# A product of values and output weights taken in 16-bit parts that POOL splits off, with a ring of two for masked blocks

## What is computed

```python
q = causal_conv_silu(x @ Wq); k = causal_conv_silu(x @ Wk)      # (b, t, 16, 128), then normalised
v = causal_conv_silu(x @ Wv)                                     # (b, t, 16, 256)
def step(state, inp):                                            # over the positions t
    qt, kt, vt, at, bt = inp
    state = state * at
    err = vt - einsum('bhkv,bhk->bhv', state, kt)
    state = state + bt * einsum('bhk,bhv->bhkv', kt, err)
    return state, einsum('bhkv,bhk->bhv', state, qt)
out = outs.reshape(b, t, 4096) @ Wo                              # 4096 = 16 heads x 256 values
x = x + out
```

## Time and profile before

| what | value |
|---|---|
| median of 3 runs | 1176.99 us |
| lowest, highest | 1175.23, 1182.03 us |
| profiled execution, its own time | 1187.94 us |
| span of its trace | 1186.1 us |
| mean granted TensorE clock | 0.945 |
| busy PE, DVE, ACT, POOL | 1057.7, 844.3, 721.0, 442.2 us |
| share of the span | 89%, 71%, 61%, 37% |

### The profile page before, as it was taken

One profiled execution on the slowest core, in us unless ns is written; L12 is line 12 of the kernel. 1 busy time (PEld: TensorE's weight loads), 2 busy tenths in 40 slices (PEclk: granted clock), 3 DMA queues, 4 the chain that ended last, 5 costly groups with the idle time before them and its releaser, 6 DMA issues.

```text
span 1186.1 us, 24906 instructions
## 1 busy us (share of the span) xinstructions
PE 1057.7 (89%) x8176; PEld 714.3 (60%) x8176; DVE 844.3 (71%) x1427; ACT 721.0 (61%) x1284; POOL 442.2 (37%) x574
## 2 busy tenths in 40 slices
PE   3589999999999999999899999998887889996987
PEld 3257777777777776777677677776554334443444
DVE  4768888877888877888688788877544656663354
ACT  3367777777776776767677676776332345555221
POOL 5254544535445453553435355436201122223000
PEclk9889999999999999999999999999997679998788
DMA  6002000010000000000000100000000040000001
GB/s 182 20 1 63 2 28 28 1 28 0 27 27 1 27 0 27 27 0 27 3 28 1 28 27 0 10 1 1 1 1 1 1 75 1 2 2 22 1 1 36
DMA packets 30359, 22.44 MB, mean 19 GB/s; under 512 B 3014, under 2 KB 29318, under 8 KB 30139
## 3 DMA queue, kind: packets, MB, share of 16 engines
q1 hardware_dynamic: 27547, 16.89, 4.9%
q0 software_dynamic: 2720, 4.42, 1.8%
HBM read 22.94 MB, written 1.05 MB: 20 GB/s over the span
## 4 chain that ended last, share of the span: by engine, by line
PE 61%; DVE 13%; ACT 12%; issue 10%; POOL 1%; DVEq 1%; DMA 1%; SPq 0%; ACTq 0%; POOLq 0%
PE psum L1121 10%; PE psum L1179 5%; DVE y L877 4%; PE psum L1147 4%; PE psum L1260 4%; PE psum L1298 3%; PE psum L1273 3%; PE psum L1199 3%; ACT L648 2%; PE psum L1137 2%; PE psum L1207 2%; PE psum L1457 2%; ACT kq L648 2%; ACT sq L651 2%; DVE ux L842 2%
## 5 line engine op out<-in xcount | busy, mean ns | idle before, releaser
L434 POOL TENSOR_TENSOR ct<-lm,levels 128x512 f16<-128x512 f32 x224 | 253.1, 1160 | 261.1 <-DVE lm L887 261.1
L877 DVE SCALAR_TENSOR_TENSOR y<-psum,cwh,y 128x508 f32<-128x508 f32 (+2 forms) x384 | 284.4, 741 | 17.6 <-ACT y L604 8.6
L842 DVE TENSOR_TENSOR ux<-ux,psum 128x512 f16<-128x512 f16 x192 | 130.7, 681 | 46.5 <-PE psum L1208 46.4
L1137 PE MATMUL psum<-wo,vt 128*128 128x256 f32 x512 | 127.4, 393 | 1.9 <-DVE y L877 1.4
L604 ACT ACTIVATE y<-psum,cwh 128x512 f32<-128x512 f32 x128 | 99.0, 774 | 37.7 <-PE psum L1121 37.7
L579 ACT ACTIVATE t1c<-psum 128x256 f16<-128x256 f32 x192 | 73.1, 380 | 63.0 <-PE psum L1199 61.9
L724 ACT ACTIVATE et<-psum 128x1024 f32<-128x1024 f32 x64 | 65.6, 1025 | 62.6 <-PE psum L1442 62.5
L1137 PEld LDWEIGHTS psum<-wo,vt 128*128 128x128 f32 x512 | 94.5, 195 | 12.8 <-DVE y L877 1.6
L991 DVE TENSOR_REDUCE mx<-psum 128x4 f32<-128x1024 f32 x64 | 77.7, 1221 | 28.8 <-PE psum L1421 28.6
L1199 PE MATMUL psum<-ux,ct 128*128 128x128 f16 x768 | 97.5, 221 | 0.6 <-ACT t1c L579 0.6
L856 DVE TENSOR_TENSOR ux<-ux,psum 128x512 f16<-128x512 f16 x128 | 87.6, 685 | 14.3 <-PE psum L1208 11.8
(11 more groups left out here) (209 smaller groups left out, 2346.0 us busy)
## 6 DMA issues: line engine op xcount, KB each, us to landing
wraw<-in_L_attn_Wv SPq DMA_DIRECT2D x32, 128.0 KB, 2.7
wo<-in_L_attn_Wo SPq DMA_DIRECT2D x16, 256.0 KB, 2.8
wraw<-in_L_attn_Wk SPq DMA_DIRECT2D x16, 128.0 KB, 2.5
wraw<-in_L_attn_Wq SPq DMA_DIRECT2D x16, 128.0 KB, 2.7
x<-in_x SPq DMA_DIRECT2D x8, 128.0 KB, 5.2
maskrow<-in_mask_row POOLq DMA_DIRECT2D x1, 1024.0 KB, 4.6
xt<-in_ctx SPq DMA_DIRECT2D x1, 1024.0 KB, 6.0
out<-x SPq DMA_DIRECT2D x8, 128.0 KB, 1.8
```

The source lines that it names most:

```text
L434: g.tensor_tensor(ct[:, st.c % 4, l], lm[:, st.c % 4, :, 0, :], levels[:, l, :].unsqueeze(1).to_broadcast([P, NB, T]), ALU.mult).then_inc( ...
L842: v.tensor_tensor(u, u, pr, ALU.subtract).then_inc(uxb_sb, 1)
L877: v.scalar_tensor_tensor(out=y[:, n, :, sh:], in0=u[:, :, 0:T - sh], scalar=cwh[:, (a.c // 2) % 2, n, TAPS - 1 - sh:TAPS - sh], in1=y[:, n ...
L1137: mm = t.matmul(ubank[n][:, j * H:(j + 1) * H], vt[:, r, vc, (2 * n + j) * T:(2 * n + j + 1) * T], wo[:, hr, vc, :], start=(vc == 0), stop ...
```

## The change

- A new POOL helper `split_wo` (three operations of 128 x 512) scales the weights `wo` by 64 and splits them into `woh` and `wol`, 16 bits each. It runs in odd slots, once for a head.
- A new POOL helper `split_v` (two operations of 128 x 1024) splits `vt` of step b0 into `vth` and `vtl`. It runs in every slot. Both stand behind `parts` and `split`, and ahead of the cuts of levels 4 to 6.
- `z(n)` makes three 16-bit products (`vth` x `woh`, `vth` x `wol`, `vtl` x `woh`) in place of each 32-bit one. It waits for `v_split` and `wo_split` in place of `silu` and the load. `zcopy` scales by 1/64.
- `vt` has one place in place of two: `v_silu` of a step waits for `split_v` of the step before. `ct` has two places in place of four: a cut waits for level 6 of two steps before.
- SP's load of `wo` waits for `wo_split` of the head two before, in place of z.

```diff
--- before.py
+++ after.py
@@ -181,9 +181,13 @@
         whi = lb("whi", [P, 2, TILES, CH, P], F16)
         wlo = lb("wlo", [P, 2, TILES, CH, P], F16)
         wo = lb("wo", [P, 2, 2, H], F32)
+        woh = lb("woh", [P, 2, 2, H], F16)
+        wol = lb("wol", [P, 2, 2, H], F16)
         y = lb("y", [P, TILES, NB, T], F32)
         kq = lb("kq", [P, 2, NB, 2, T], F32)
-        vt = lb("vt", [P, 2, 2, TOK], F32)
+        vt = lb("vt", [P, 2, TOK], F32)
+        vth = lb("vth", [P, 2, 2, TOK], F16)
+        vtl = lb("vtl", [P, 2, 2, TOK], F16)
         sq = lb("sq", [P, NB, 2, T], F32)
         n2m = lb("n2m", [P, 2, NB], F32)
         lnn = lb("lnn", [P, 2, NB], F32)
@@ -193,7 +197,7 @@
         rows = lb("rows", [P, P], BF16)
         decay = lb("decay", [P, NB, 2, T], F32)
         lm = lb("lm", [P, 4, NB, 2, T], F32)
-        ct = lb("ct", [P, 4, LEVELS, NB, T], F16)
+        ct = lb("ct", [P, 2, LEVELS, NB, T], F16)
         ux = lb("ux", [P, 2, NB, 2, T], F16)
         t1b = lb("t1b", [P, NB, T], F16)
         t1c = lb("t1c", [P, NB, T], F16)
@@ -280,6 +284,7 @@
         x0_full, res_psum, res_sb, y0_psum, y0_sb, y_psum, y_sb, out_psum, added = [sem(n) for n in (
             "x0_full", "res_psum", "res_sb", "y0_psum", "y0_sb", "y_psum", "y_sb", "out_psum", "added")]
         z_psum, z_sb = sem("z_psum"), sem("z_sb")
+        v_high, v_split, wo_high, wo_split = [sem(n) for n in ("v_high", "v_split", "wo_high", "wo_split")]
 
         xdone, result = sem("xdone"), sem("result")
         kv_names = ("ctx_loaded", "ctx_masked", "mask_cast", "mask_ready", "bias_cast", "bias_ready", "k_psum", "k_high", "k_stack", "v_psum", "v_ready")
@@ -362,7 +367,7 @@
                         need(sp, w_split, nxt.head)
                         load_w(nxt.head)
                         if nxt.c // 2 >= 2:
-                            sp.wait_ge(z_psum, nxt.at(-4).count(2, 4))
+                            sp.wait_ge(wo_split, nxt.head - 1)
                         load_wo(nxt.head, (nxt.c // 2) % 2)
 
             slots(sp, slot)
@@ -418,6 +423,30 @@
                 pool.wait_ge(w_high, h * 2 + 2)
                 g.tensor_tensor(wlo[:, ring].rearrange("p n c t -> p (n c t)"), w, wh, ALU.subtract).then_inc(w_split, 1)
 
+            def split_wo(st):
+
+                h, ring = st.head, (st.c // 2) % 2
+                pool.wait_ge(wo_loaded[ring], 16 * (st.c // 4 + 1) if st.i is None else st.i * 16 + 16 * (st.c // 4 + 1))
+                need(pool, z_psum, st.at(-4).count(2, 4))
+                w = wo[:, ring].rearrange("p v n -> p (v n)")
+                wh, wl = [q[:, ring].rearrange("p v n -> p (v n)") for q in (woh, wol)]
+                g.tensor_tensor(w, w, c64[:].to_broadcast([P, 2 * H]), ALU.mult).then_inc(wo_high, 1)
+                pool.wait_ge(wo_high, h * 2 + 1)
+                g.tensor_tensor(wh, w, zero[:].to_broadcast([P, 2 * H]), ALU.add).then_inc(wo_high, 1)
+                pool.wait_ge(wo_high, h * 2 + 2)
+                g.tensor_tensor(wl, w, wh, ALU.subtract).then_inc(wo_split, 1)
+
+            def split_v(st):
+
+                if not st.valid():
+                    return
+                pool.wait_ge(silu, st.count(2, 2))
+                need(pool, z_psum, st.at(-2).count(2, 2))
+                f, hi, lo = vt[:].rearrange("p v n -> p (v n)"), vth[:, st.c % 2].rearrange("p v n -> p (v n)"), vtl[:, st.c % 2].rearrange("p v n -> p (v n)")
+                g.tensor_tensor(hi, f, zero[:].to_broadcast([P, 2 * TOK]), ALU.add).then_inc(v_high, 1)
+                pool.wait_ge(v_high, st.count(1, 1))
+                g.tensor_tensor(lo, f, hi, ALU.subtract).then_inc(v_split, 1)
+
             pool.wait_ge(conv_scaled, 3)
             pool.wait_ge(xn_done, B)
             split(0, 0, None)
@@ -429,9 +458,9 @@
                     if not st.valid():
                         return
                     pool.wait_ge(lm_done, st.count(2, 2))
-                    need(pool, t1c_psum, st.at(-4).count(6, 6))
+                    need(pool, t1c_psum, st.at(-2).count(6, 6))
                     for l in levels_:
-                        g.tensor_tensor(ct[:, st.c % 4, l], lm[:, st.c % 4, :, 0, :],
+                        g.tensor_tensor(ct[:, st.c % 2, l], lm[:, st.c % 4, :, 0, :],
                                         levels[:, l, :].unsqueeze(1).to_broadcast([P, NB, T]), ALU.mult).then_inc(masked, 1)
 
                 cut(b, range(2, 4))
@@ -450,6 +479,9 @@
                     nxt = k.at(4)
                     first = k.i is None and k.c <= -2
                     split(nxt.head, (nxt.c // 2) % 2, None if first else nxt.at(-4))
+                if k.c % 2 == 1 and b0.valid():
+                    split_wo(b0)
+                split_v(b0)
                 cut(b, range(4, LEVELS))
                 cut(b0, range(0, 2))
                 if k.i is None and k.c == STEPS - 3:
@@ -471,6 +503,7 @@
             pool.wait_ge(squared, STEPS)
             pool.wait_ge(masked, STEPS * LEVELS)
             pool.wait_ge(w_split, HK)
+            pool.wait_ge(z_psum, STEPS * 2)
             pool.wait_ge(v_psum, B)
             pool.wait_ge(k_stack, 2 * B)
             pool.wait_ge(bias_ready, 1)
@@ -593,7 +626,7 @@
                     if b.valid():
                         act.wait_ge(z_psum, b.count(2, n + 1))
                         need(act, out_psum, b.at(-2).count(2, 2))
-                        s.activation(zz[:, b.c % 2, 2 * n:2 * n + 2], ubank[n].rearrange("p (j n) -> p j n", j=2), ACT.Copy).then_inc(z_sb, 1)
+                        s.activation(zz[:, b.c % 2, 2 * n:2 * n + 2], ubank[n].rearrange("p (j n) -> p j n", j=2), ACT.Copy, scale=1.0 / WSCALE).then_inc(z_sb, 1)
 
                 def bias(n):
                     if a.valid():
@@ -654,8 +687,8 @@
                     if not a.valid():
                         return
                     act.wait_ge(tapped, a.count(12, 12))
-                    need(act, z_psum, a.at(-2).count(2, 2))
-                    s.activation(vt[:, a.c % 2], y[:, 2:4].rearrange("p a j t -> p a (j t)"), ACT.Silu).then_inc(silu, 1)
+                    need(act, v_split, a.count(1, 0))
+                    s.activation(vt[:], y[:, 2:4].rearrange("p a j t -> p a (j t)"), ACT.Silu).then_inc(silu, 1)
 
                 def k_split(n):
 
@@ -1130,11 +1163,15 @@
                     if k.i is None and k.c == STEPS - 1:
                         pe.wait_ge(v_ready, NB * 2)
                     if n == 0:
-                        pe.wait_ge(silu, b.count(2, 2))
-                        pe.wait_ge(wo_loaded[hr], 16 * (b.c // 4 + 1) if b.i is None else b.i * 16 + 16 * (b.c // 4 + 1))
+                        pe.wait_ge(v_split, b.count(1, 1))
+                        pe.wait_ge(wo_split, b.head + 1)
                     for j in range(2):
+                        o = ubank[n][:, j * H:(j + 1) * H]
                         for vc in range(2):
-                            mm = t.matmul(ubank[n][:, j * H:(j + 1) * H], vt[:, r, vc, (2 * n + j) * T:(2 * n + j + 1) * T], wo[:, hr, vc, :], start=(vc == 0), stop=(vc == 1))
+                            toks = slice((2 * n + j) * T, (2 * n + j + 1) * T)
+                            t.matmul(o, vth[:, r, vc, toks], woh[:, hr, vc, :], start=(vc == 0), stop=False)
+                            t.matmul(o, vth[:, r, vc, toks], wol[:, hr, vc, :], start=False, stop=False)
+                            mm = t.matmul(o, vtl[:, r, vc, toks], woh[:, hr, vc, :], start=False, stop=(vc == 1))
                     mm.then_inc(z_psum, 1)
 
                 def norms():
@@ -1186,7 +1223,7 @@
                     pe.wait_ge(masked, b.count(7, 1))
                     need(pe, uxb_sb, b.count(8, hf))
                     for jj in range(2):
-                        cj = ct[:, b.c % 4, 0, 2 * hf + jj]
+                        cj = ct[:, b.c % 2, 0, 2 * hf + jj]
                         t.matmul(bx[:, jj * 256:jj * 256 + P], ident16[:], cj, start=True, stop=True)
                         mm = t.matmul(bx[:, jj * 256 + P:jj * 256 + 256], cj, ident16[:], start=True, stop=True)
                     mm.then_inc(uxb_psum, 1)
@@ -1196,7 +1233,7 @@
                     pe.wait_ge(masked, st.count(7, level + 1))
                     need(pe, sb_sem, st.count(6, n - 1))
                     for jj in range(2):
-                        mm = t.matmul(dst[:, jj * P:(jj + 1) * P], ct[:, st.c % 4, level, 2 * hf + jj], ux[:, st.c % 2, 2 * hf + jj, 1], start=True, stop=True)
+                        mm = t.matmul(dst[:, jj * P:(jj + 1) * P], ct[:, st.c % 2, level, 2 * hf + jj], ux[:, st.c % 2, 2 * hf + jj, 1], start=True, stop=True)
                     mm.then_inc(psum_sem, 1)
 
                 def both(st, hf, dst, t1s, sb_sem, n, x_sem, x_n, psum_sem):
```

## The result

The changed kernel took 1208.83 us (median of 4 runs, 1204.23 to 1212.7) against 1179.51 us of the kernel before in the same set (4 runs, 1175.23 to 1191.79). The ratio is 1.023, with a 95% interval of 1.0143 to 1.0316: some 27 us slower, where no change was forecast. The profiled execution took 1212.7 us with a span of 1210.9, so 24.8 us more than the profiled one of before on either count.

What follows compares the result with a forecast made beforehand. The prediction took a 24.56 us chain of waits through ACT, DVE and PE, without z, as the bound. Slots 0 and 1 (+2.6), a turn (-0.4) and the end (-2.0) gave +0.2, so 1177.2 us, range 1163 to 1188.

Steps and rivals of the forecast that it cites:

- the rhythm: Steady step, norms to norms, 24.56 us: z is not on its chain, so the shorter z counts 0.
- POOL's prices and cover: POOL's added splits: split_v 4.05 us, split_wo 2.9 to 3.4, hidden by POOL's wait for lm, cost 0.
- the start: Slots 0 and 1: POOL delays b_first(0) in slot 1, PE runs slow behind it; together +2.6 us.
- slot 0's gain of 0.75: z(0) in slot 0, at PE's half rate: 2.58 us instead of 3.33, a gain of 0.75.
- the end: Last slots: four groups of z on the chain, 0.49 us saved each, -2.0 us in all.
- the loop's turns: Loop's worst turn: z(0) runs slow after a PE gap of 4.19 us; shorter z gains 0.4 us.
- the loop's turns cost more: Rival at six loop turns: longer PE and POOL lists, each 0 to 4.2 us dearer, up to 1202; chance 0.06.
- a shorter z(0) makes that wait longer and nothing else: PE before norms: already waits 0.23 us for ACT's squares, so a shorter z(0) only lengthens that wait, gain 0.

Runs made afterwards that it cites:

- e4: Changed kernel with all 35 slots written out and no loop on any engine: 1172.03 us, ratio 0.9872 to the kernel before.
- e5: Kernel before with all 35 slots written out and no loop on any engine: 1155.49 us, ratio 0.9783.
- e8: Kernel before with 64 small matmuls that nothing reads ahead of PE's program, loop body untouched: 1207.51 us, ratio 1.0217.
- e7: Changed kernel with its loop and a fourth product of z (vtl x wol): 1205.02 us, ratio 1.0192.
- e9: Changed kernel with 32 small unread matmuls ahead on PE, loop body 64 instructions further on: ratio 1.02 to the kernel before.
- e10: Changed kernel with 64 small unread matmuls ahead on PE, loop body 128 instructions further on: ratio 1.0332 to the kernel before.
- e6: Changed kernel without a loop, with a fourth product of z (vtl x wol): 1164.82 us, ratio 0.9822 to the kernel before.
- e13: Kernel before with 128 small unread matmuls at PE's start, loop body 256 instructions further on: ratio 1.0036.
- e3: Kernel before with all of POOL's new splits and ct in two places, z in 32 bits but waiting for the splits: 1191.14 us, ratio 1.0073.
- e1: Changed kernel without the third product of z (vtl x woh): 1222.89 us, ratio 1.0267 to the kernel before.

## Why the prediction was wrong

- **Right: the rhythm.** z was counted 0 in the 24.56 us step. Between turns, `norms` to `norms` is still 24.55 us at full clock, and without a loop the slots at full clock take 24.33 us in e4, with the shorter z, as in e5.
- **Right: POOL's prices and cover.** `split_v` 1.894 + 2.133 = 4.03 us (4.05 said), `split_wo` 3.23 us (2.9 to 3.4), waits for `lm` 0.44 and 3.65 us (0.3 and 3). The taps on DVE stayed at a median of 742 ns against 741.
- **Right in kind, near in size by luck: the start.** +2.6 was said for slots 0 and 1, slot 0's gain of 0.75 included, and +1.9 measured. But slot 1 ends anywhere between 121.4 and 128.3 us in the profiled executions of the kernel before at its six places, so one pair of executions cannot confirm such a term. `b_first(0)` of slot 1 waits for POOL, at half clock behind it, as said. PE's timeline:

```profile
68.48 0.23 PE L1227 MATMUL psum<-ct,ident 128*128 128x128 f16 x1 [2.63 <-POOL ct L463]
...
70.18 1.95 PE L1184 MATMUL psum<-ones,sq 128*128 128x1 f32 x16
...
90.77 0.29 PE L1227 MATMUL psum<-ct,ident 128*128 128x128 f16 x1 [3.92 <-POOL ct L463]
...
91.17 0.42 PE L1172 MATMUL psum<-woh,vth 128*128 128x256 f16 x1
```

But it starts at 90.77 and not 92.5. After slot 0's wait of 2.63 us PE kept its full clock this time (`norms` at 70.18, 1.7 us behind `b_first`), so z(0) took 1.3 us there, not the 3.33 of the earlier trace rows and not the 2.58 forecast.
- **Not decided: the end.** -2.0 was said, and what follows the 27 slots is 4.2 us shorter. But that stretch takes 377.9 to 387.7 us in the kernel before at its six places and 371.9 to 384.6 in the changed one at four, so the 4.2 is no measure of the 2.0.
- **Wrong, the step that failed: the loop's turns.** The sum has "-0.4 at a turn", from the one slow turn of the earlier trace rows taken as it stood. That row's "issue" was the fetch of a body that was usually kept; the change makes it happen at five turns, and each brings its half-clock stretch. A fetched turn makes the slot 5.1 us longer on average (32.06 in e8, all five fetched, against 26.94, the mean of the four that were not in the kernel before), and the five slots of e8 are together 160.3 - 138.2 = 22.1 us longer, most of its 2.2%. The changed kernel pays +14.3 us in these slots, less than 4 x 5.1. Its shorter z is not the reason, as e7 with a full-length z pays 13.5; at its other places the changed kernel pays 11.0 (e9) to 27.4 (e10), so the price of a fetch seems to depend on the place as well. The rival "the loop's turns cost more" had the mechanism, the place and a time, up to 1202, but a chance of 0.06.
- **Wrong: "a shorter z(0) makes that wait longer and nothing else".** The longer wait has a price, by e4 against e6 and the changed kernel against e7: the 22 slots without a turn are 12.8 us longer than before, and 10.7 longer than in e7, at the lower clock. From 100 to 820 us PE spends 78 us at the lower level, before 14; about half of the 78 lies in the slots with a turn and half in the others. With that, PE's busy time fell by 2.5 us and not by 30.

**Still open.** Why the kernel before fetches its body at one turn, the one of the earlier trace rows, and e13 at the same one; and why e3 and e1 fetch at two and three, although their loop begins at the same place and has the same number of matmuls. By the traces their turn has one instruction of the sequencer more (249 against 248), which would matter at the edge of a narrow place, but no run tests it. What sets off the lower clock is not shown beyond the kernels compared. Nor is it shown why e7's profiled execution (1191.7) lay so far below its median (1205.02).

**The version to use** is neither: e5, the kernel before with its loop written out, at 0.9783 (0.9733 to 0.9832) of before. By the traces it saves the fetched turn, the 2.4 us that even a kept turn costs over 24.56, and 0.23 us a step, some 21 us of the 28 in the medians. z in 16-bit parts on top of it (e4) brings nothing.

## What to carry to other kernels

A runtime loop on a full engine can be a bet on its instruction memory, as it was here: look at the instruction queue's packets in the middle of the loop, and at "issue" waits where it turns, before adding an instruction to its body or ahead of it. A body that just fits can cost 2% for a change that touches none of its timing, so compare a variant with one that only shifts the program. And work taken from an engine that isn't the bound is worth nothing if it leaves a wait in front of the next piece: the clock may fall, and with it the work on the path.

## What the runs showed that was not expected

- The loop body stays or is fetched according to its place modulo 256 instructions, 16.4 KB: q8 46 packets at 0, 55 at 32, 83 at 64, 128 and 192, 47 at 256.
- A fetched turn is 9 packets and a gap of about 3.3 us on PE (16.3 / 5, the changed kernel), and with the stretch at 1.2 GHz behind it 5.1 us of the slot (e8 against before).
- The trace names the wrong releaser for such a gap: POOL, which was done long before. The weight loads' row has it right.
- PE at 97% busy kept a clock of 1.00 in all windows from 200 to 800 us (e6); with one product less in z and 94 to 95% busy it had 0.93 to 0.98 (e4). The share alone does not settle it: e7 was 93.4% busy at 1.00 from 500 to 600 us.
